# Power attention layer: the repeated, unread decay product is left out

## The chip, the core and the metric

One core of one Trainium2 chip. The metric is the time of one execution on the device in microseconds (us), the median of several; lower is better. The core has five engines that run side by side: TensorE (PE in the profile; PEld is its weight load), VectorE (DVE), ScalarE (ACT), GpSimd (POOL) and SyncE (SP, which here only issues DMAs). They wait for each other through semaphores.

## What is computed

Four layers one after the other on 16 batches of 256 tokens with 128 features: softmax attention with 16 heads, a gated mixture of 8 experts with its own attention, a "power" attention, and a capped mixture of 7 experts. The change touches the third alone:

```python
S = einsum('bhtd,bhsd->bhts', Q, K)                  # 16 heads of 8 features
Tm = 2 * log(abs(S) + EPS) + log(scale)              # power 2 of the score
Z = Tm + log_G[..., :, None] - log_G[..., None, :]   # decay: sums of log-sigmoid gates
Z = where(tril, Z, -inf)
P = exp(Z - rowmax(Z)); norm = sum(P)
O = einsum('bhts,bhsd->bhtd', P, V) / norm
x = x + layernorm(O)
```

## The kernel before, in words

The power layer (`power_layer`) goes through its batches in sixteen steps t = 0 to 15 (NB is 16), and each step through eight units u = 0 to 7 of two heads; n = 8 t + u numbers the units. A unit works on tiles of 128 x 512 elements of near blocks (keys in the same 128 tokens as the query) and 128 x 256 of far ones:

- TensorE forms the logarithms of the decays in one of two banks `decay_ps`: `decays(n)` (L1542, L1543) first writes a mask into the whole bank (a product of the identity in `cstb` with the causal mask `late`, both bf16), and `near_blocks(n)` (L1560) adds four small products of 32 rows, row differences of the cumulated gates, between them the near scores (L1564) in `score_ps`. `far_scores(n)` (L1578) adds the far ones.
- ACT takes the exponential of the bank into one of four buffers `E` (L1235).
- DVE takes the absolute value of the scores into `A` (L1419), 768 columns at once, and ACT squares it into `PT` (L1223). The squares stand for the exponential of 2 log|S|.
- POOL multiplies the near part of `PT` with `E` (L993).
- TensorE multiplies the weights with the values (`times_v`, L1597), two units at a time, and DVE copies the sums out (`OS`, L1317). They are turned (L1516) and normed.

TensorE's order in a unit is: `far_scores(n)`, `decays(n + 1)`, `near_blocks(n + 1)`, then what `POWER_AT` puts there for other batches (turning, projections, cumulated gates, router), `times_v`, and guests. `far_scores(n)` and `near_blocks(n + 1)` wait until DVE has taken the scores of unit n - 1; `decays(n + 1)` waits until ACT has read its bank two units ago. Each engine works in the order in which its code is written. The guests are the end of the layer before (gathers on POOL, sums on DVE, norms on ACT), spread over steps 0 to 10.

In `decays`, the product that writes the mask is made more than once in most steps: once more in steps 0 to 9, not in steps 10 to 13, twice more in steps 14 and 15. Each of these products starts a new accumulation (`start=True`) in the same bank, with the same operands, so that the next one overwrites it and nobody reads it.

Of the kernel before, what the change touches and what calls it, by code (L numbers as in the profile page):

```python
# [40 lines left out]
P = 128  # L41
NB, S, D = 16, 256, 128
# [791 lines left out]
def power_layer(nc, low, weighted_in, top, take, X, cst, cstb, QK, Vx, w, Y, chosen, router, bias, yd, wi, wo, gated, dram):  # L834
# [2 lines left out]

    NU, NE, NA, NW, WD, WU = H // 2, 4, 4, 12, 4 * P, 6 * P
    EXPERTS, EARLY, END = 7, (NB - 3) * TC, NB - 1
    STEPS, AGAIN, EARLY_CS = range(NB + 5), 2, 2  # L840
    UNITS = gated.UNITS
    with ExitStack() as ctx:
        def sb(name, shape, dt):
# [3 lines left out]
        def pb(name, banks):  # L847
            return ctx.enter_context(nc.psum_tensor(f"{name}P", [P, banks, 512], F32))
# [5 lines left out]
        decay_ps = pb("decay_ps", 2)  # L854
# [112 lines left out]
        def reach(eng, sem, count):  # L967
            if count > 0:
                eng.wait_ge(sem, count)
# [541 lines left out]
        def tensor(pe, guests):  # L1511
# [20 lines left out]
            late = cstb[:, P:2 * P].unsqueeze(1).to_broadcast([P, 4, P])  # L1532

            def decays(n):
                t, u = n // NU, n % NU
                if n < 2:
                    pe.wait_ge(gated.s_sg, UNITS - 1 + n)
                if u == 0:
                    pe.wait_ge(s_m, 96 * (t + 1))
                reach(pe, s_taken, n - 1)  # L1540
                for _ in range(AGAIN if t >= NB - 2 else t < 10):
                    pe.matmul(decay_ps[:, n % 2, :], cstb[:, 0:P], late, start=True, stop=True)  # L1542
                pe.matmul(decay_ps[:, n % 2, :], cstb[:, 0:P], late, start=True, stop=False)  # L1543

            def near_blocks(n):
# [36 lines left out]
            def times_v(t, g):  # L1582
# [16 lines left out]
                last.then_inc(s_pv, 1)  # L1599

            decays(0)
            near_blocks(0)
            guests[-1, 7]()
            for t in STEPS:
                for u in range(NU):
                    n = NU * t + u
                    if n < NU * NB:
                        far_scores(n)
                    if n + 1 < NU * NB:
                        decays(n + 1)  # L1610
                        near_blocks(n + 1)
# [1362 lines left out]
def build(nc, dram, out):  # L2974
    with ExitStack() as ctx:
# [21 lines left out]
        with ExitStack() as c1:  # L2997
# [34 lines left out]
            yd = nc.dram_tensor("tokens", [NT, D + 2], F32).ap()  # L3032
            od = nc.dram_tensor("expert_outputs", [2 * NT + P, D], F32).ap()
            power = power_layer(nc, Region(nc, front, back), weighted_in, Region(nc, small.at, region.end), take, X,
                                cst, cstb, QK, Vx, weights[2], XB, chosen, w["router1"], w["bias1"], yd, wi, wo, gated,
                                dram)
# [177 lines left out]
```

## Time and profile before

| | |
|---|---|
| time, median of 3 runs | 1105.17 us (1102.54 to 1108.28) |
| time of the profiled execution | 1104.22 us, span of its instructions 1102.3 us |
| mean granted clock of TensorE | 0.962 of full speed |
| power layer, first to last score | 670 to 951 us |
| PE busy over the span | 992.7 us (90%) |
| DVE busy | 850.8 us (77%) |
| ACT busy | 774.9 us (70%) |
| POOL busy | 637.9 us (58%) |

The profile is of one execution; its own time is the one to which sums of its rows are compared. Times in its rows are microseconds from the start of the span. Matmuls overlap in the systolic array and their ends are modelled: two that start 0.2 us apart may each last 0.4, so for TensorE the distance from start to start tells what one costs.

### The profile page before, as it was taken

The numbers are of one execution on the slowest core, as the hardware profiler recorded it, in microseconds if no ns is written. First come the engines' busy times: TensorE is split into PE (matmuls) and PEld (weight loads), VectorE is DVE, ScalarE is ACT, GpSimd is POOL, SyncE is SP. The second block draws the span as 40 slices with busy tenths as digits, with TensorE's granted clock in tenths as the row PEclk, the third lists the DMA queues.
The fourth block names the chain that finished last, engine by engine and source line by source line (L and its number), as shares of the span: only waits on it lengthen the run. The fifth ranks groups of instructions, "written<-read, shape, count | busy, mean of one in ns | idle before, by whom it ended". The sixth has DMA issues, their size and how long they took to land. (4 is left out here: it accounts for less than half of the span.)

```text
span 1102.3 us, 30949 instructions
## 1 busy us (share of the span) xinstructions
PE 992.7 (90%) x10503; PEld 586.9 (53%) x10503; DVE 850.8 (77%) x2252; ACT 774.9 (70%) x1760; POOL 637.9 (58%) x710
## 2 busy tenths in 40 slices
PE   4899999999999988988999998999999999848975
PEld 2344444444444443436998875555555565534752
DVE  3789999999999998954756767888989987772324
ACT  1578888888888877884554665788888998642405
POOL 4235544555443333760476838799888887526753
PEclk9999999999999999998999998999999999858988
DMA  5022222211111111220444421112121121141227
GB/s 133 26 58 77 77 73 77 77 55 40 41 41 40 41 33 43 59 70 20 132 124 132 134 75 41 48 43 66 44 61 32 36 58 52 40 164 41 53 74 198
DMA packets 114423, 75.24 MB, mean 68 GB/s; under 512 B 21335, under 2 KB 107808, under 8 KB 114272
## 3 DMA queue, kind: packets, MB, share of 16 engines
q1 hardware_dynamic: 105840, 54.68, 18.2%
q0 software_dynamic: 7744, 18.13, 5.5%
q8 instruction: 90, 1.47, 0.6%
q14 instruction: 61, 0.50, 0.2%
q10 hardware_dynamic: 688, 0.46, 0.1%
HBM read 26.75 MB, written 26.51 MB: 48 GB/s over the span
## 5 line engine op out<-in xcount | busy, mean ns | idle before, releaser
L637 DVE TENSOR_REDUCE mxsS<-scoreS 128x2 f32<-128x512 f32 x512 | 327.7, 685 | 40.9 <-PE scoreS L779 37.2
L519 ACT ACTIVATE PTS<-stS 128x512 f32<-128x512 f32 x512 | 284.1, 595 | 55.4 <-PE stS L783 54.2
L779 PE MATMUL scoreS<-QK 31*128 31x256 f16 x1024 | 171.6, 280 | 30.6 <-DVE mxsS L637 16.5
L993 POOL TENSOR_TENSOR PTP<-PTP,EP 128x512 f32<-128x512 f32 x128 | 163.3, 1280 | 38.7 <-ACT PTP L1223 37.7
L783 PE MATMUL stS<-QK 32*128 32x256 f16 x1024 | 169.4, 278 | 2.3 <-ACT PTS L519 2.3
L701 PE MATMUL pvS<-PTS,Vx 128*32 128x256 f32 x2048 | 142.0, 396 | 0.4 <-ACT PTS L519 0.2
L779 PEld LDWEIGHTS scoreS<-QK 31*128 31x128 f16 x1024 | 52.7, 93 | 152.6 <-DVE mxsS L637 105.5
L1419 DVE TENSOR_SCALAR AP<-score_psP 128x768 int32<-128x768 int32 x128 | 121.7, 951 | 12.1 <-PE score_psP L1578 10.6
L1223 ACT ACTIVATE PTP<-AP,epsP 128x768 f32<-128x768 f32 x128 | 118.9, 929 | 6.8 <-DVE AP L1419 6.5
L392 POOL TENSOR_TENSOR rsS<-veS,halfS 128x2 f32<-128x2 f32 (+1 forms) x32 | 33.0, 1031 | 154.0 <-DVE veS L605 87.1
L1235 ACT ACTIVATE EP<-decay_psP 128x512 f32<-128x512 f32 x128 | 75.7, 592 | 29.1 <-PE decay_psP L1560 27.4
L2175 POOL DMA_INDIRECT sorted<-gy,gidx x64 | 62.0, 969 | 41.5 <-DVE gowner L2537 22.8
L701 PEld LDWEIGHTS pvS<-PTS,Vx 128*32 128x32 f32 x2048 | 54.5, 111 | 51.0 <-issue 23.0
L2318 PE MATMUL gdown_ps<-down_w,gprod 128*128 (+1 forms) x496 | 65.7, 276 | 3.4 <-DVE XB L2573 3.1
L2318 PEld LDWEIGHTS gdown_ps<-down_w,gprod 128*128 128x128 f32 x496 | 60.1, 192 | 5.3 <-issue 4.4
L2645 DVE TENSOR_TENSOR gprod<-gsg,gup_ps 128x512 f32<-128x512 f32 x62 | 42.5, 686 | 22.2 <-ACT gsg L2430 10.9
L2187 POOL DMA_INDIRECT ggot<-mixed,gidx x48 | 46.7, 973 | 21.7 <-issue 13.3
L2367 ACT ACTIVATE ghTs<-gturn_ps,norm 128x256 f16<-128x256 f32 x46 | 21.8, 473 | 50.3 <-PE gturn_ps L2257 49.5
L783 PEld LDWEIGHTS stS<-QK 32*128 32x128 f16 x1024 | 51.9, 93 | 6.2 <-ACT PTS L519 3.1
L1560 PEld LDWEIGHTS decay_psP<-MP 32*128 32x128 bf16 x512 | 28.5, 93 | 48.6 <-issue 44.1
L398 POOL TENSOR_SCALAR yS<-X,mvS,rsS 128x128 f32<-128x128 f32 x64 | 50.6, 797 | 1.7
L1564 PE MATMUL score_psP<-QK 31*128 31x128 f16 x512 | 50.6, 218 | 0.0
(399 smaller groups left out, 2310.7 us busy)
## 6 DMA issues: line engine op xcount, KB each, us to landing
QK<-HLS SPq DMA_DIRECT2D x384, 32.0 KB
QK<-HLP SPq DMA_DIRECT2D x192, 32.0 KB
gsin<-sorted SPq DMA_DIRECT2D x46, 128.0 KB
mixed<-gob SPq DMA_DIRECT2D x46, 128.0 KB
sorted<-ggot POOLq DMA_DIRECT2D x22, 256.0 KB, 2.7
expert_outputs<-tzero SPq DMA_DIRECT2D x8, 512.0 KB
cgot<-expert_outputs SPq DMA_DIRECT2D x16, 256.0 KB, 5.4
tokens<-XB SPq DMA_DIRECT2D x16, 128.0 KB
```

Of the source, the lines that this page charges most:

```text
L398: last = pool.tensor_scalar(y[:, c, :], rows_of(X, b)[c], mv[:, c, 0:1], rs[:, kind, c:c + 1], ALU.subtract, ALU.mult)
L519: act.activation(PT[:, n % NPT, :], st_ps[:, (NS * t + n) % 3, :], ACT.Exp, scale=SCALE).then_inc(s_exp, 1)
L637: dve.tensor_reduce(mxs[:, u // 4, :, at], score_ps[:, n % 2, :].rearrange("p (c s) -> p c s", c=TC), AX.X, ALU.max).then_inc(s_max, 1)
L701: last = pe.matmul(pv_ps[32 * j:32 * j + 32, q], Vx[:, t % 3, c, 4 * g + j, :], PT[:, (4 * g + (j ^ 2)) % NPT, S * c:S * c + S], start=(c ...
L779: scored = pe.matmul(score_ps[:, k, cols], QK[part, new, g, 0, rows], QK[part, new, g, 1, :], start=True, stop=True)
L783: turned = pe.matmul(st_ps[:, (NS * t + n) % 3, cols], QK[part, old, g, 1, rows], QK[part, old, g, 0, :], start=True, stop=True)
L993: eng.tensor_tensor(w, w, E[:, n % NE, :], ALU.mult).then_inc(s_wd if n % NU in MULT_BY_DVE else s_wp, 1)
L1223: act.activation(PT[:, n % NW, :], A[:, n % NA, :], ACT.Square, bias=eps[:, 0:1]).then_inc(s_sq, 1)
L1235: act.activation(E[:, n % NE, :], decay_ps[:, n % 2, :], ACT.Exp).then_inc(s_taken, 1)
L1419: dve.tensor_scalar(A[:, n % NA, :].bitcast(I32), score_ps[:, n % 2 * WU:n % 2 * WU + WU].bitcast(I32), 0x7FFFFFFF, None, ALU.bitwise_and) ...
L2175: pool.indirect_dma_start(tables[h], bass.IndirectOffsetOnAxis(ap=idx[h][:, c, t:t + 1], axis=0), y[:, tiles[h].start + t, :], None).then_ ...
L2318: last = pe.matmul(down_ps[:, x % 2, t * D:(t + 1) * D], prod[:, x % NPROD, c * SLOTS + t * P:c * SLOTS + (t + 1) * P], down_flat[:, colum ...
```

## The change

The additional mask products are no longer issued, in whatever step; the one that starts the accumulation stays. The constant that told their number goes too.

```diff
-    STEPS, AGAIN, EARLY_CS = range(NB + 5), 2, 2
+    STEPS, EARLY_CS = range(NB + 5), 2
...
             def decays(n):
                 t, u = n // NU, n % NU
...
                 reach(pe, s_taken, n - 1)
-                for _ in range(AGAIN if t >= NB - 2 else t < 10):
-                    pe.matmul(decay_ps[:, n % 2, :], cstb[:, 0:P], late, start=True, stop=True)
                 pe.matmul(decay_ps[:, n % 2, :], cstb[:, 0:P], late, start=True, stop=False)
```

On TensorE, a unit in one of the first ten steps, before the change. `cstb` is the mask product's identity, `MP` the gates' rows:

```order
L1578 MATMUL score_psP<-QK 128x128 x2
L1542 MATMUL decay_psP<-cstb 128x512
L1543 MATMUL decay_psP<-cstb 128x512
L1560 MATMUL decay_psP<-MP 128x128
L1564 MATMUL score_psP<-QK 128x128
```

Such a row of L1542 stands there 80 times. On TensorE again, the first unit of step 14 in the program, before, with the values' product ahead of it:

```order
L1597 MATMUL pvP<-PTP,VkP 32x128 x4
L1578 MATMUL score_psP<-QK 128x128 x2
L1542 MATMUL decay_psP<-cstb 128x512 x2
L1543 MATMUL decay_psP<-cstb 128x512
L1560 MATMUL decay_psP<-MP 128x128
```

And the same place of the changed program, whose lines behind the edit have moved up by two (L1541 is the old L1543):

```order
L1595 MATMUL pvP<-PTP,VkP 32x128 x4
L1576 MATMUL score_psP<-QK 128x128 x2
L1541 MATMUL decay_psP<-cstb 128x512
L1558 MATMUL decay_psP<-MP 128x128
L1562 MATMUL score_psP<-QK 128x128
```

Only the rows of L1542 are gone, 80 single ones and 16 double ones, 112 products. Nothing else stands elsewhere on any engine.

## Rows read from the trace of the kernel before

**Rows 1.** The page, part 2: granted clock in 40 slices, tenths.

```profile
PEclk9999999999999999998999998999999999858988
```

**Rows 2.** Windows by step (1 to 6, 11, 13, 14, 15): length, then busy us (instructions) of PE, PEld, DVE, ACT, POOL; clock, DMA, GB/s.

```profile
692.41:709.70 17.29, 15.85 (x205) 8.75 (x197) 15.33 (x32) 14.39 (x31) 14.09 (x12) 1.00 0.11 29
709.70:726.53 16.83, 16.83 (x223) 9.45 (x223) 14.18 (x33) 14.00 (x30) 15.49 (x15) 1.00 0.20 52
726.53:743.81 17.28, 16.96 (x223) 9.44 (x223) 16.28 (x47) 15.27 (x35) 16.14 (x17) 1.00 0.20 50
743.81:762.13 18.32, 17.71 (x229) 10.09 (x229) 15.60 (x40) 16.62 (x39) 17.19 (x17) 1.00 0.21 56
762.13:780.98 18.85, 18.40 (x238) 10.32 (x237) 17.16 (x47) 15.96 (x35) 16.60 (x16) 1.00 0.21 53
780.98:798.37 17.39, 17.08 (x225) 9.87 (x220) 16.38 (x50) 15.08 (x35) 15.73 (x16) 1.00 0.21 56
...
870.11:886.28 16.17, 16.07 (x221) 9.95 (x220) 14.63 (x40) 14.76 (x35) 13.07 (x13) 1.00 0.14 36
...
902.52:918.92 16.40, 16.30 (x223) 10.08 (x223) 14.26 (x35) 15.54 (x34) 14.10 (x13) 1.00 0.20 53
918.92:936.36 17.44, 17.44 (x227) 9.46 (x227) 13.84 (x33) 13.45 (x27) 12.30 (x11) 1.00 0.22 61
936.36:950.71 14.35, 14.35 (x202) 7.73 (x202) 11.14 (x26) 11.67 (x21) 10.47 (x11) 1.00 0.10 24
```

**Rows 3.** Groups of TensorE's instructions by line and shape: count, busy us, mean ns.

```profile
L1543 PE MATMUL decay_psP<-cstb 128*128 128x512 bf16 x128 | 49.1, 384 | 0.0
...
L1542 PE MATMUL decay_psP<-cstb 128*128 128x512 bf16 x112 | 41.2, 392 | 0.0
```

**Rows 4.** TensorE in order of time, first unit of step 7: start, length in us.

```profile
798.05 0.28 PE L1578 MATMUL score_psP<-QK 31*128 31x128 f16 x2
798.26 0.39 PE L1542 MATMUL decay_psP<-cstb 128*128 128x512 bf16 x1
798.49 0.38 PE L1543 MATMUL decay_psP<-cstb 128*128 128x512 bf16 x1
...
800.29 0.28 PE L1578 MATMUL score_psP<-QK 31*128 31x128 f16 x2
```

**Rows 5.** The same of step 11, which has no repeated product.

```profile
869.79 0.28 PE L1578 MATMUL score_psP<-QK 31*128 31x128 f16 x2
870.01 0.39 PE L1543 MATMUL decay_psP<-cstb 128*128 128x512 bf16 x1
...
871.82 0.28 PE L1578 MATMUL score_psP<-QK 31*128 31x128 f16 x2
```

**Rows 6.** TensorE in order of time: far scores of step 0, and two of step 7.

```profile
682.63 0.28 PE L1578 MATMUL score_psP<-QK 31*128 31x128 f16 x2 [3.48 <-DVE AP L1419]
...
684.89 0.39 PE L1578 MATMUL score_psP<-QK 31*128 31x128 f16 x2 [0.91 <-DVE AP L1419]
...
689.42 0.39 PE L1578 MATMUL score_psP<-QK 31*128 31x128 f16 x2
...
811.70 0.28 PE L1578 MATMUL score_psP<-QK 31*128 31x128 f16 x2 [0.61 <-DVE AP L1419]
...
814.69 0.28 PE L1578 MATMUL score_psP<-QK 31*128 31x128 f16 x2
```

**Rows 7.** Windows around changes of the clock, columns as in rows 2.

```profile
382.99:386.40 3.41, 2.26 (x24) 1.14 (x26) 1.92 (x6) 1.82 (x5) 0.00 (x0) 1.00 0.18 50
386.40:389.81 3.41, 3.41 (x31) 1.68 (x30) 2.83 (x5) 2.44 (x5) 0.00 (x0) 0.50 0.03 9
...
683.36:690.19 6.83, 5.92 (x53) 3.17 (x52) 3.43 (x10) 3.96 (x9) 6.18 (x7) 0.50 0.10 25
...
864.27:867.68 3.41, 2.19 (x24) 1.51 (x27) 2.90 (x6) 2.98 (x5) 3.41 (x4) 1.00 0.06 14
```

**Rows 8.** Waits in the power layer: who waited for whom, us in total, times, longest.

```profile
PE score_psP L1578 <- DVE AP L1419: 9.9, 14, 3.5
```

## The prediction

> **What bounds the kernel now.** The first view is the page's second part, for TensorE's clock [rows 1]: it is whole in the slices of the power layer but for the one in which the layer starts, and low behind its end. The windows by step [rows 2] give each step's length and what each engine was busy in it; steps 7 to 9 repeat steps 4 to 6 to within 0.05 us. TensorE is busy nearly all of each step (17.71 of 18.32 us in step 4), but so are its modelled ends, and DVE, ACT and POOL stand at 15.60 to 17.19 in the same step. So shares alone don't tell who sets the pace. The order in time does: in step 7 the product of a far score starts at 798.05 and the next one at 800.29, a unit of 2.24 us [rows 4]; in step 11, in which no product is repeated, the same unit takes from 869.79 to 871.82, 2.03 us [rows 5]. The 0.21 us between them is the repeated product. TensorE thus sets the pace in this unit and would in the others as long as nobody else is late. Somebody else is, now and then: TensorE waited for DVE's absolute values 14 times in the layer, 9.9 us [rows 8], 3.48 us of it at once in step 0 [rows 6].
>
> **What the change removes.** 112 products of 128x512: ten steps of eight units with one, two steps with two, and the rows by line count the 112 [rows 3]. Nothing is moved and no wait is added; DVE, ACT, POOL and the DMA queues get the same instructions. The product left behind it clears the bank for the accumulation as before.
>
> *Price of one.* Not its 392 ns [rows 3], which overlap with the next one: start to start it is 798.26 to 798.49, 0.23 us [rows 4], and the two units above differ by 0.21. I take 0.21. If every one counted, 112 x 0.21 = 23.5 us; six of the eight in step 0 don't, since DVE is behind there (the waits of 3.48 and 0.91 us) [rows 6]. Upper bound of the gain: 106 x 0.21 = 22.3 us.
>
> (The Trainium skill, "TensorE: Matmul & The Clock Gate", section Back-to-back issue gap, gives 131 ns for each product of 512 columns in a sustained stream. By it the 112 would be 14.7 us instead of 23.5. This trace doesn't agree: its products of 512 columns start 230 ns apart.)
>
> *What takes over.* A step can't be shorter than its busiest in-order engine plus what that engine waits. The steps without the product show that rest: step 13 took 16.40 us with ACT busy 15.54, 0.86 above; step 11 took 16.17 with ACT busy 14.76, 1.41 above, and there TensorE still set the pace [rows 2]. So 0.86 is the better floor, and 1.41 the cautious one. I count DVE and ACT; POOL may fall up to four units behind (four decay buffers), and its mean over steps 1 to 6, 15.9 us, is below all floors but that of step 2. New length = the larger of (length - products x 0.21) and (busiest + 0.86):
> - step 1: 17.29, floor 15.33 + 0.86 = 16.19: gain 1.10
> - step 2: 16.83, floor 15.04, TensorE alone 16.83 - 1.68 = 15.15: gain 1.68
> - step 3: floor 16.28 + 0.86: gain 0.14
> - step 4: 18.32, ACT 16.62 + 0.86 = 17.48: 0.84; step 5: 18.85, DVE 17.16 + 0.86 = 18.02: 0.83; step 6: 17.39, DVE 16.38 + 0.86: 0.15. Steps 7 to 9 the same. Together 3.64
> - step 14 (two products a unit, 16 x 0.21 = 3.36 at most): 17.44, floor 13.84 + 0.86 = 14.70: 2.74
> - step 15: 14.35, ACT 11.67 + 0.86 = 12.53: 1.82
> - step 0: the two units in which TensorE was ahead: 0.4.
>
> Sum 11.5 us. With 1.41 for 0.86 the same sum is 0.55 + 1.24 + 0 + 2 x (0.29 + 0.28 + 0) + 2.19 + 1.27 + 0 = 6.4 us. Between 6.4 and 22.3 I take 11.5: the floors of four engines that lean on each other are seldom beaten.
>
> *Does it arrive at the end?* Behind the layer the last batch is routed and sorted before the experts can start; nothing there has a fixed time, so I pass the gain on whole. Where the low clock behind the layer ends may shift against the work, a us or two either way.
>
> *The clock.* The product also kept TensorE busy. In this trace the clock fell at 386.40 after 3.41 us of which TensorE was busy 2.26, and came back 3.41 us later [rows 7]; it fell at 683.36 after the 3.48 us wait and stayed at 0.50 (1.2 of 2.4 GHz) for 6.83 us [rows 6, 7]. In step 10, without a repeated product, TensorE was busy only 2.19 of 3.41 us (from 864.27) and the clock stayed [rows 7]. Both outcomes for about the same load: the steps that will look like step 10 (4 and 7, which have the same guests) are near the edge, while steps 11 and 13 ran without the product at 1.00 throughout. The price of a stretch of 3.41 us at half speed: a unit of step 0 took 4.53 us in the low clock (684.89 to 689.42) against 2.99 in step 7 (811.70 to 814.69), 0.34 us per us, 1.16 a stretch [rows 6]; at most half the stretch, 1.7. The unit of step 7 held four more transposes, so I take 1.5. I expect two such stretches more than now: 3.0 us back.
>
> Forecast: 11.5 - 3.0 = 8.5 us less than the 1104.2 of the profiled execution: 1095.7. That execution lies 1 us below the median shown; against this the same gain gives 1096.7, well inside the range.
>
> **The rivals.**
> - *TensorE alone was the bound.* All four engines slide together and nearly every product counts: 106 x 0.21, less a us or two of clock: 1082 to 1089, the middle 1084. For it: units repeat to 0.01 us between steps, as rows 4 and 5 show for one, though DVE is busy 91% of step 5. Against it: DVE 17.16 and ACT 16.62 leave no room for 1.68 us less in steps 5 and 4. Chance 0.10.
> - *Another wait takes the place.* The floor is 1.41, the gain 6.4, and two to four stretches of low clock take most of it: 1100.8, within 1099.7 to 1110.7. For it: steps 3, 6 and 9 are only 1.0 above DVE already. Chance 0.20.
> - *The clock falls again and again: slower.* The idle stretches are now a fifth of a us longer in every unit in which TensorE waits for DVE. If it fell once in each of the sixteen steps: 16 x 1.5 = 24, less 11.5: 1116.7. It decides from eight falls (8 x 1.5 = 12 > 11.5), and it is slower by over 0.5% from twelve. For it: the load before the fall at 386.40 was that of step 10. Against it: steps 11 and 13 never lost it, since TensorE, being the bound, closes up when a product goes. Chance 0.20.
> (The Trainium skill, the same page, section on the clock gate, says that the throttled state is the default and activity releases it, and so speaks against taking out filler work. By this rule the fall at 683.36 agrees, and the whole clock in step 11 shows that the filler isn't needed everywhere.)
> - *Forecast,* 1089 to 1099.7: chance 0.50.
>
> **How the numbers follow.** A measurement of this kernel tells 0.5% (5.5 us) from no change. Faster by more: 0.50 + 0.10 less the edges, 0.59. Within: 0.21. Slower by more: 0.20. The range reaches from 1085 (half of the first rival is left out) to 1111 (most of the third is): 0.05 + 0.15 outside. The forecast's own range is 1089 to 1099.7.
>
> **What the profile will show.** Right: the unit of rows 4 takes 2.03 us or a little more; steps 4 to 9 are 0.1 to 0.9 us shorter, steps 14 and 15 together 4.5; DVE's and ACT's idle times before their power lines shrink and TensorE's waits for DVE grow over 9.9 us; the windows show at most three more stretches at 0.50. Wrong: if steps 4 to 9 lose 1.7 us each, the floors were false; if clock below 1.00 stands in most steps, the price was the product's other use; if the steps shorten and the end doesn't, something behind the layer has a time of its own.

## The result and the profile after

| | before | changed |
|---|---|---|
| time, median of 19 runs each | 1104.0 us (1101.84 to 1111.08) | 1112.71 us (1102.34 to 1122.33) |
| ratio, 95% interval | | 1.0053 [1.0034, 1.0071] |
| profiled execution | 1104.22 us, span 1102.3 | 1122.33 us, span 1120.4 |
| its mean granted clock | 0.962 | 0.932 |

The kernel became slower by half a per cent, where 1095.7 us was forecast and 1111 was the upper end. The changed kernel spreads over 20 us from run to run, twice as much as before, and its time goes with the granted clock: 1102.34 us at 0.951, 1112.71 at 0.940, 1122.33 at 0.932. The profiled execution is the slowest of the 19, so more of it was lost to the low clock than usual; the changed kernel was therefore profiled again (below, the run called "Again"), with four of the five falls in the same places. The ratios leave out executions over 1.5% above the fastest of their kernel, here that slowest one and one of the kernel before beside the last four experiments (1213.88 us at a clock of 0.744). This ratio isn't the quotient of the two medians, which is 1.0079.

The page of the changed kernel, first part and the clock in 40 slices, beside [rows 1]:

```profile
span 1120.4 us, 30725 instructions
PE 1000.6 (89%) x10391; PEld 598.3 (53%) x10391; DVE 855.4 (76%) x2252; ACT 777.4 (69%) x1760; POOL 637.2 (57%) x710
...
PEclk9999999999999998979999998799696799958988
```

TensorE has fewer instructions and is busy for longer, 1000.6 us against 992.7. That can't be work; it is the same work at a lower clock. Slices 26, 29, 31 and 32, in the power layer, hold new digits below 9. The windows by step, of steps 0, 1, 3, 5, 6, 9, 10, 11, 14 and 15, with the columns of [rows 2]:

```profile
672.17:694.63 22.46, 15.01 (x163) 8.38 (x162) 19.51 (x41) 13.39 (x24) 19.62 (x18) 0.85 0.14 37
694.63:716.65 22.02, 21.02 (x182) 12.23 (x182) 14.53 (x33) 14.73 (x31) 12.96 (x11) 0.61 0.11 27
...
731.99:750.84 18.85, 16.92 (x215) 10.56 (x214) 16.32 (x48) 16.30 (x36) 18.36 (x18) 0.91 0.18 48
...
768.12:787.71 19.59, 17.90 (x255) 10.96 (x254) 18.83 (x47) 16.90 (x37) 18.54 (x17) 1.00 0.23 58
787.71:811.68 23.97, 22.97 (x186) 13.48 (x186) 16.74 (x49) 15.71 (x35) 15.66 (x15) 0.57 0.17 42
...
848.53:872.93 24.40, 23.40 (x186) 13.82 (x186) 16.76 (x50) 16.20 (x35) 13.63 (x13) 0.55 0.11 28
872.93:894.17 21.24, 20.02 (x221) 12.07 (x220) 15.91 (x40) 15.80 (x37) 14.27 (x13) 0.79 0.10 25
894.17:910.33 16.16, 16.05 (x221) 9.95 (x220) 14.62 (x40) 14.47 (x34) 12.00 (x12) 1.00 0.13 33
...
942.54:957.55 15.01, 14.08 (x211) 8.53 (x210) 13.69 (x34) 13.92 (x28) 11.54 (x12) 1.00 0.26 68
957.55:970.32 12.77, 11.52 (x187) 6.84 (x186) 11.05 (x26) 11.86 (x22) 10.69 (x10) 1.00 0.14 35
```

The sixteen steps take 298.15 us; before they took 279.94. The difference of 18.2 is that of the two executions (1122.33 - 1104.22 = 18.1), so as good as the whole of it arose in this layer (which starts 1.4 us later, and what is behind it is 1.5 shorter). Two kinds of steps are to be told apart. Steps 14 and 15 are 4.0 us shorter than before (27.78 against 31.79 [rows 2]), and step 11, which lost nothing, takes what it took. Steps 1, 6, 9 and 10 are 4 to 7 us longer, and their clock reads 0.55 to 0.79. Step 5 stands apart: its clock is whole, and yet it is 0.74 longer than in [rows 2], with DVE busy 18.83 us instead of 17.16 (step 8 is its copy, 19.58).

The stretches of low clock and those between them, by windows, beside [rows 7]:

```profile
697.60:714.70 17.10, 17.10 (x148) 10.09 (x147) 10.10 (x21) 11.07 (x24) 11.96 (x10) 0.50 0.07 19
714.70:745.40 30.70, 28.66 (x402) 16.98 (x396) 28.54 (x76) 26.06 (x54) 27.17 (x26) 1.00 0.19 50
745.40:748.80 3.40, 3.40 (x36) 2.81 (x36) 1.66 (x5) 3.15 (x9) 3.40 (x4) 0.50 0.10 24
...
789.80:810.30 20.50, 20.50 (x160) 12.10 (x158) 13.34 (x41) 13.75 (x32) 14.25 (x14) 0.50 0.16 39
...
851.20:878.50 27.30, 27.30 (x221) 15.67 (x220) 18.52 (x54) 18.04 (x40) 15.55 (x15) 0.50 0.11 29
...
888.70:892.10 3.40, 3.40 (x36) 2.80 (x36) 1.52 (x4) 3.17 (x9) 3.40 (x5) 0.51 0.15 37
```

Together 71.7 us at 0.50, where before there was none behind 690.19. In them TensorE is busy without a gap and in the three long ones DVE, ACT and POOL are busy 57 to 70% of the time: there TensorE, at 1.2 GHz, alone sets the pace. What stands ahead of the falls? TensorE in order of time, its far scores with the wait before them, and at the end the unit that answers to [rows 4]:

```profile
695.63 0.28 PE L1576 MATMUL score_psP<-QK 31*128 31x128 f16 x2 [1.89 <-DVE AP L1419]
...
788.71 0.28 PE L1576 MATMUL score_psP<-QK 31*128 31x128 f16 x2 [1.79 <-DVE AP L1419]
...
811.36 0.28 PE L1576 MATMUL score_psP<-QK 31*128 31x128 f16 x2
...
813.39 0.28 PE L1576 MATMUL score_psP<-QK 31*128 31x128 f16 x2
```

At full clock the unit takes 2.03 us, as forecast. Behind step 0 TensorE waits for DVE for more than 1.1 us seven times: in step and unit 1/1 (1.89), 3/5 (1.25), 4/6 (1.23), 6/1 (1.79), 7/6 (1.22), 9/1 (1.78) and 10/6 (1.22). Each of the five falls follows one of them within 2.5 us: 1/1, 3/5, 6/1, 9/1 and 10/6. Before, behind step 0, only one wait was that long (10/6). For the whole layer the row of [rows 8] (9.9 us) becomes 20.6; then the same row from 690 us to the layer's end, changed and before:

```profile
PE score_psP L1576 <- DVE AP L1419: 20.6, 22, 4.3
...
PE score_psP L1576 <- DVE AP L1419: 14.9, 18, 1.9
...
PE score_psP L1578 <- DVE AP L1419: 5.3, 11, 1.2
```

Why is DVE 1.8 us late at 6/1? DVE and then POOL in order of time at the end of step 5, changed kernel:

```profile
785.27 2.52 DVE L2584 SCALAR_TENSOR_TENSOR XB<-ggot_late,gW,XB 128x128 f32<-128x128 f32 x2
787.71 0.94 DVE L1419 TENSOR_SCALAR AP<-score_psP 128x768 int32<-128x768 int32 x1
...
785.07 2.57 POOL L993 TENSOR_TENSOR PTP<-PTP,EP 128x512 f32<-128x512 f32 x2
```

And the same place before:

```profile
780.13 0.92 DVE L2586 SCALAR_TENSOR_TENSOR XB<-ggot_late,gW,XB 128x128 f32<-128x128 f32 x2
780.98 0.94 DVE L1419 TENSOR_SCALAR AP<-score_psP 128x768 int32<-128x768 int32 x1
...
779.36 1.28 POOL L993 TENSOR_TENSOR PTP<-PTP,EP 128x512 f32<-128x512 f32 x1
781.04 1.28 POOL L993 TENSOR_TENSOR PTP<-PTP,EP 128x512 f32<-128x512 f32 x1 [0.40 <-ACT PTP L1223]
```

The two sums are guests, the end of the layer before (block 6 here, block 7 in step 8). Before, POOL had a gap between two products in which the second sum ran in 0.34 us. Now the product that ACT releases comes earlier, POOL works through without a gap, and the two sums take 2.52 us together, as long as POOL's two products in the same time. DVE takes the next scores 1.6 us later, and TensorE waits.

The long wait at 1/1 has the same cause. DVE, POOL in order of time at the start of step 1, changed kernel:

```profile
692.44 2.19 DVE L2584 SCALAR_TENSOR_TENSOR XB<-ggot,gW,XB 128x128 f32<-128x128 f32 x4
...
693.21 1.27 POOL L993 TENSOR_TENSOR PTP<-PTP,EP 128x512 f32<-128x512 f32 x1 [0.54 <-ACT PTP L1223]
```

And the same place before:

```profile
691.29 1.13 DVE L2586 SCALAR_TENSOR_TENSOR XB<-ggot,gW,XB 128x128 f32<-128x128 f32 x4
...
692.48 1.27 POOL L993 TENSOR_TENSOR PTP<-PTP,EP 128x512 f32<-128x512 f32 x1 [1.47 <-ACT PTP L1223]
```

Before, the four sums were over when POOL's product began; now they meet it and take 1.06 us longer, and TensorE's wait at 1/1 grows from 0.61 to 1.89.

### The profile page after: what moved, and what is told of

Same layout as the page of the kernel before. It is cut to its first block and busy times, and to the rows that moved or that the text cites. A ratio compares the mean times of both kernels' runs of the same rounds, so it can differ in the third digit from the quotient of the medians.

```text
span 1120.4 us, 30725 instructions
## 1 busy us (share of the span) xinstructions
PE 1000.6 (89%) x10391; PEld 598.3 (53%) x10391; DVE 855.4 (76%) x2252; ACT 777.4 (69%) x1760; POOL 637.2 (57%) x710
## 3 DMA queue, kind: packets, MB, share of 16 engines
q8 instruction: 89, 1.46, 0.5%
## 5 line engine op out<-in xcount | busy, mean ns | idle before, releaser
L1576 PE MATMUL score_psP<-QK 31*128 31x128 f16 x256 | 38.2, 232 | 21.3 <-DVE AP L1419 20.6
L1562 PE MATMUL score_psP<-QK 31*128 31x128 f16 x512 | 54.7, 231 | 0.0
L1558 PE MATMUL decay_psP<-MP 32*128 32x128 bf16 x512 | 54.6, 231 | 0.0
```

Source lines behind the costliest of these rows:

```text
L1562: pe.matmul(score_ps[:, o:o + P], QK[band, t % 3, g, 1, rows], QK[band, t % 3, g, 0, rows], start=True, stop=True)
```

## The experiments

The theories, after the result. *The clock:* the time is lost to long stretches at half speed, each set off by one wait of TensorE for DVE, and the sums that collide with POOL's products make the two most costly ones. *A fixed cost per step:* the repeated product served a timing in every step, so its return anywhere gives the time back. *Not the clock:* DVE and POOL collide more, and the low clock is only a sign of that. Each diff is against the changed kernel, except that a loop returned is shown alone. The first four were timed beside the kernel before on one chip, the next four on a second and the last four on a third, so each is to be judged by its ratio to the kernel before.

**Late part alone** (product kept in steps 0 to 9, gone in 14 and 15).

```diff
+                for _ in range(t < 10):
+                    pe.matmul(decay_ps[:, n % 2, :], cstb[:, 0:P], late, start=True, stop=True)
```

> The repeated product stays in steps 0 to 9 and goes in steps 14 and 15 only. Theory A (the time was lost because TensorE's clock fell in steps 0 to 10, and only there): 4.5 us faster than before, about 1099.5, no stretch of low clock in the power layer beyond the one at its start, steps 14 and 15 at about 15.0 and 12.6 us. Theory B (a product less costs the clock wherever it is left out): stretches of low clock in steps 14 and 15, no gain or slower, 1104 to 1108.

Measured: 1099.4 us against 1104.44, ratio 0.9949 [0.9923, 0.9975]. Steps 14 and 15 by windows:

```profile
924.18:939.19 15.01, 14.08 (x211) 8.53 (x210) 13.69 (x33) 13.93 (x28) 11.56 (x12) 1.00 0.25 67
939.19:951.99 12.80, 11.53 (x187) 6.84 (x186) 11.06 (x27) 11.88 (x22) 10.73 (x10) 1.00 0.14 33
```

They are those of the changed kernel to 0.03 us. This part of the change is a gain of 4.0 us in the two steps and 5.0 by the medians (5.6 by the ratio), and arrives at the end. In one point theory A missed: the clock also fell at 871.8, for 3.4 us, behind the wait of 1.23 us at 10/6, where the program is that of before.

**Early part alone** (gone in steps 0 to 9, kept twice in 14 and 15).

```diff
+                for _ in range(AGAIN if t >= NB - 2 else 0):
+                    pe.matmul(decay_ps[:, n % 2, :], cstb[:, 0:P], late, start=True, stop=True)
```

> The repeated product goes in steps 0 to 9 and stays, twice, in steps 14 and 15. Theory A: slower than before by the loss of the whole change plus the 4.5 us that steps 14 and 15 gave, so 1110 to 1120, with low clock in several of steps 0 to 10. Theory B: the loss is shared, 1106 to 1108.

Measured: 1117.07 us, ratio 1.0080 [1.0047, 1.0114]. The early part carries the whole loss. Its profile shows the pair of sums at 1226 and 1357 ns, and 54.6 us at half clock in the layer behind 690, in five stretches, one of them behind each collision: 789.2 to 799.4 and 847.2 to 867.7.

**One more** (two additional products in steps 0 to 9 and in 14, 15: 80 more than before).

```diff
+                for _ in range(AGAIN if t >= NB - 2 or t < 10 else 0):
+                    pe.matmul(decay_ps[:, n % 2, :], cstb[:, 0:P], late, start=True, stop=True)
```

> One more product than before in steps 0 to 9 (two repeated ones), else as before: the price of one product while the clock is whole. Theory A (each costs TensorE, which sets the pace, 0.21 us): 80 x 0.21 = 17 us slower, about 1121, and the clock no worse than before. Theory C (the product is half hidden behind other engines' work): 5 to 9 us slower. If the product gives back clock even here, less than 5.

Measured: 1120.62 us, ratio 1.0124 [1.0091, 1.0157]. 16.2 us for 80 products is 0.20 each (by the ratio 13.7 us, 0.17 each), and a unit of step 4 takes 2.46 us (two products more than the 2.03 of [rows 5]):

```profile
750.05 0.28 PE L1578 MATMUL score_psP<-QK 31*128 31x128 f16 x2
750.26 0.61 PE L1542 MATMUL decay_psP<-cstb 128*128 128x512 bf16 x2
...
752.51 0.28 PE L1578 MATMUL score_psP<-QK 31*128 31x128 f16 x2
```

The price of a product holds. The sums collide here as well (935 and 1357 ns), yet the clock shows no fall in the layer behind 692. TensorE's waits behind step 0 are shorter there than in the changed kernel, 1.27 us at the most; whether that or the products themselves kept the clock, this run doesn't tell.

**Without the colliding sums.** The second half of the second sum of blocks 6 and 7 is left out of the computation (unit 7 of steps 5 and 8), and the first half gives the signal that the sum is ready.

```diff
-            if some.stop == TB:
+            if some.stop == (2 if c == 1 and b in range(EARLY, 8) else TB):
...
-                    after.update({(t, 3): tail(("add0a", b)), (t, 4): tail(("add0b", b)), (t, 6): tail(("add1a", b)),
-                                  (t, 7): tail(("add1b", b))})
+                    after.update({(t, 3): tail(("add0a", b)), (t, 4): tail(("add0b", b)), (t, 6): tail(("add1a", b))})
```

> The changed kernel, and the second half of the second sums of the last two blocks of the layer before (two operations of DVE in unit 7 of steps 5 and 8, each) is left out of the computation. In the changed kernel they took 2.5 us against 0.92 before, while POOL worked through two power products, and TensorE then waited 1.8 us before its clock fell in step 6 and in step 9. Theory D (that pile-up sets off the two long falls): no low clock from step 6 unit 1 to step 10 unit 0, a stretch of 40 to 48 us less at half speed, 1095 to 1104. Theory E (a lower load as such makes the clock fall, here or a little later): the falls stay, a few us at most below the changed kernel, 1108 to 1114.

Measured: 1095.69 us, ratio 0.9900 [0.9869, 0.9930]. Four sums gone, 2 us of DVE's work at the pace of before, make 17 us of difference to the changed kernel. Windows from the first fall on:

```profile
692.80:706.50 13.70, 13.03 (x102) 7.05 (x106) 8.91 (x20) 9.65 (x21) 8.22 (x7) 0.50 0.07 19
706.50:863.40 156.90, 146.48 (x2008) 89.78 (x2001) 146.57 (x385) 142.28 (x314) 142.00 (x132) 1.00 0.20 50
863.40:866.80 3.40, 3.40 (x35) 2.42 (x34) 1.06 (x3) 2.97 (x8) 3.40 (x5) 0.51 0.16 40
```

The long falls of steps 6 and 9 are gone. This takes work away, though; the next run only moves it.

**The sums moved** one unit ahead, nothing left out.

```diff
-                    after.update({(t, 3): tail(("add0a", b)), (t, 4): tail(("add0b", b)), (t, 6): tail(("add1a", b)),
-                                  (t, 7): tail(("add1b", b))})
+                    after.update({(t, 3): tail(("add0a", b)), (t, 4): tail(("add0b", b)), (t, 6): tail(("add1a", b), ("add1b", b))})
```

> The changed kernel with all its work; the second half of those sums stands one unit earlier on DVE (unit 6 of steps 5 and 8), where in the changed kernel's trace POOL runs operations of one input. Theory D (the pile-up of those sums with POOL's products sets off the long falls): the sums take 0.3 to 0.5 us each, steps 6 and 9 keep the clock, 1096 to 1103. Theory E (leaving the work out had lowered DVE's load, and that alone helped): at least one of the two falls stays, 1108 to 1114.

Measured: 1098.38 us against 1103.98, ratio 0.9944 [0.9920, 0.9969]. A sum takes 371 or 340 ns in unit 6, and steps 6 and 9 keep the clock. Falls remain at 694.2 (13.7 us), 813.7 (3.4) and 940.0 (10.2). The one of 3.4 gives a price: unit 7/6 takes 4.09 us with it, and 4/6, the same unit of a step with the same guests, 2.78 without, 1.3 us. The one at 940.0 has no long wait ahead of it: TensorE had waited 0.27 us at 939.66.

**The sums moved, and the product back in steps 0 and 1.**

```diff
+                for _ in range(t < 2):
+                    pe.matmul(decay_ps[:, n % 2, :], cstb[:, 0:P], late, start=True, stop=True)
```

> As the kernel before: sums one unit earlier, and the repeated product in steps 0 and 1 only. If the product in step 1 is what keeps the clock from 697 us on, the low stretch of 13.7 to 17.1 us that followed there in the runs without it is gone: 2 to 5 us faster than with the sums moved alone, about 1094. If the fall there comes anyway, no difference to the sums moved alone.

Measured: 1097.67 us, ratio 0.9940 [0.9925, 0.9955], no different from the run before. The fall at the start came anyway, at 698.4 (10.2 us); two more are at 742.8 (6.8) and 852.0 (3.4). A miss: the product in these units doesn't protect step 1. What stands ahead of the fall is again a collision, of another guest: an operation of DVE on four columns, which took 0.16 us before and runs beside POOL's product here. DVE, then POOL:

```profile
694.17 1.25 DVE L2607 SCALAR_TENSOR_TENSOR gnm<-gmv,grs 128x4 f32<-128x4 f32 x1
...
694.11 1.29 POOL L993 TENSOR_TENSOR PTP<-PTP,EP 128x512 f32<-128x512 f32 x1 [1.27 <-ACT PTP L1223]
```

TensorE then waited 1.71 us at 1/1.

**Half a product** (256 columns in steps 0 to 9).

```diff
+                for _ in range(t < 10):
+                    pe.matmul(decay_ps[:, n % 2, 0:2 * P], cstb[:, 0:P], late[:, 0:2, :], start=True, stop=True)
```

> Steps 0 to 9 repeat half of the product (256 columns), steps 14 and 15 nothing. If the price goes by columns and the clock holds: 80 x 0.105 = 8.4 us less than with the whole product there (1099.4 measured), limited by DVE's and ACT's floors to 3 to 6: 1093 to 1096. If half doesn't keep the clock or the sums pile up as in the changed kernel: 1105 to 1114.

Measured: 1103.85 us, ratio 0.9993 [0.9963, 1.0022]. The sums still collide (1225 and 1367 ns), and the falls behind them are at 783.5 (6.8 us) and 841.5 (10.2); a third, at 872.2 (3.4), follows the wait at 10/6. Half the product, shorter stretches, no gain in the end.

**The product in two steps alone** (5 and 8, those of the collisions; the sums not moved).

```diff
+                for _ in range(t in (5, 8)):
+                    pe.matmul(decay_ps[:, n % 2, :], cstb[:, 0:P], late, start=True, stop=True)
```

> The repeated product in steps 5 and 8 alone, the sums where they were. Theory D with timing (the product keeps TensorE slow enough there that POOL isn't behind when the sums come): the pair of sums takes 0.9 to 1.2 us, the falls in steps 6 and 9 are gone, 1098 to 1105. Theory E (it takes a load in all steps): falls elsewhere, 1108 to 1114.

Measured: 1101.03 us, ratio 0.9965 [0.9938, 0.9992]. The pair is fast again, 660 and 340 ns:

```profile
783.69 0.92 DVE L2586 SCALAR_TENSOR_TENSOR XB<-ggot_late,gW,XB 128x128 f32<-128x128 f32 x2
```

Behind the first 13.7 us, two stretches of 3.4 us remain, at 797.5 and 852.1, in steps 6 and 9 after all, behind waits of 0.80 us and 0.3 us. The two long ones are gone. The product's use in these steps was the rhythm: with it, POOL's gap meets the second sum. The median is 11.7 us below that of the changed kernel; by the two ratios it is 0.0088 x 1104 = 9.7 us.

**Products only where TensorE waits** (the changed kernel with 41 unread products ahead of the far scores of the seven units that wait over 1.1 us; the sums collide as before).

```diff
+            FILL = {(1, 1): 7, (3, 5): 5, (4, 6): 5, (6, 1): 7, (7, 6): 5, (9, 1): 7, (10, 6): 5}
...
+                    if FILL.get((t, u)):
+                        reach(pe, s_taken, n)
+                        for _ in range(FILL[t, u]):
+                            pe.matmul(decay_ps[:, (n + 1) % 2, :], cstb[:, 0:P], late, start=True, stop=True)
```

> The changed kernel, with 41 unread products put only where its TensorE waited over 1.1 us for DVE: seven ahead of the far scores of units 1/1, 6/1 and 9/1, five at 3/5, 4/6, 7/6 and 10/6 (step/unit), less than the wait each. Nothing else is touched, so the waits themselves and the pile-up of the sums stay. Theory F (it is TensorE's idleness in those seven waits that makes the clock fall): no low clock between 690 and 955 us but for an odd stretch of 3.4, 1093 to 1099. Theory G (the mean load per step decides): long falls as in the changed kernel, 1108 to 1115.

Measured: 1097.67 us against 1104.82, ratio 0.9933 [0.9912, 0.9954]. TensorE and DVE in order of time at 6/1, and step 6 by windows:

```profile
777.97 1.68 PE L1609 MATMUL decay_psP<-cstb 128*128 128x512 bf16 x7
...
779.81 0.28 PE L1576 MATMUL score_psP<-QK 31*128 31x128 f16 x2 [0.15 <-DVE AP L1419]
...
776.37 2.51 DVE L2589 SCALAR_TENSOR_TENSOR XB<-ggot_late,gW,XB 128x128 f32<-128x128 f32 x2
...
778.80:796.03 17.23, 15.48 (x190) 9.13 (x188) 16.23 (x49) 14.36 (x33) 14.34 (x14) 1.00 0.21 54
```

DVE is as late as in the changed kernel (2.51 against 2.52 us), and the far scores don't start sooner for it; but the wait is filled, 0.15 us of it are left, the clock stays whole and the step takes 17.23 us instead of 23.97. Only two stretches of 3.4 us remain in the layer, at 826.6 and 833.4, behind waits of 0.4 to 0.8 us that weren't filled. This tells the clock from the collision: step 5, with the collision and a whole clock, takes 19.56 us, 1.9 more than without the collision (17.70 in the next run), and in step 6 the low clock had cost 23.97 - 17.23 = 6.7.

**The sums moved and the waits filled** (35 products by the list below and by the trace; the expectation miscounts them as 37). The loop of the run before and the edit of "the sums moved" stand beside this list.

```diff
+            FILL = {(1, 1): 7, (3, 5): 5, (4, 6): 4, (6, 0): 2, (6, 5): 3, (7, 6): 4, (9, 0): 2, (9, 5): 3, (10, 6): 5}
```

> The same idea on the kernel with the sums one unit earlier, 37 products in its own waits. By theory F the best version: no long fall, the sums 0.3 to 0.5 us each, 1090 to 1095. By theory G as with the sums moved alone, 1098.

Measured: 1093.75 us, ratio 0.9893 [0.9872, 0.9915], faster than both kernels. The layer from 692.80 to 942.00 by windows, then steps 1, 5 and 6 of it:

```profile
692.80:942.00 249.20, 240.98 (x3283) 145.89 (x3278) 229.98 (x589) 226.67 (x490) 218.59 (x202) 1.00 0.19 50
...
695.83:711.30 15.47, 14.62 (x186) 8.58 (x183) 14.13 (x31) 14.38 (x31) 12.92 (x12) 1.00 0.11 28
761.53:779.23 17.70, 16.72 (x223) 10.12 (x222) 16.94 (x48) 16.04 (x36) 16.73 (x16) 1.00 0.26 60
779.23:796.70 17.47, 16.93 (x224) 10.16 (x223) 16.42 (x50) 15.38 (x36) 16.11 (x16) 1.00 0.23 57
```

There is no low clock in it at all. The sixteen steps take 269.24 us, 10.7 less than before.

**Again** (the changed kernel once more).

> The changed kernel once more, on the chip of the others, as it is. Its pair of sums in steps 5 and 8 takes 2.5 us again if the order of the engines sets it and not chance; the low clock behind units 1/1, 6/1 and 9/1 is then seen again, 1105 to 1115.

Measured: 1110.3 us (1107.36 to 1115.92), ratio 1.0051 [1.0029, 1.0072]. In its profiled execution (1115.05 us) four of the five falls stand in the same places, with other lengths; behind the wait of 1.28 us at 3/5 none came. The windows of three:

```profile
786.00:806.50 20.50, 20.50 (x160) 12.10 (x158) 13.39 (x41) 13.75 (x32) 14.31 (x14) 0.50 0.15 39
847.50:857.70 10.20, 10.20 (x79) 6.07 (x83) 7.91 (x24) 6.54 (x17) 5.92 (x6) 0.50 0.07 21
878.20:885.00 6.80, 6.80 (x58) 4.51 (x56) 3.52 (x8) 4.37 (x11) 5.40 (x6) 0.50 0.15 39
```

With the 13.7 us at 693.9 it has 51.2 us at half clock against 71.7, and is 7.3 us faster. What differs between these two executions is above all how long the clock stays low.

**Half a product, and the sums moved.** The edits of the two runs of these names together.

> Half of the product (256 columns) in steps 0 to 9, nothing in 14 and 15, and the sums one unit earlier. In the run with half the product the sums had taken 2.6 us again and the clock fell in steps 6 and 9, 1103.9. Theory D: without the pile-up it doesn't, and the half price shows: 1094 to 1097. If the half product itself is too little for the clock: 1100 or more.

Measured: 1093.95 us, ratio 0.9895 [0.9874, 0.9915], as good as the filled waits. Low clock only at 681.7 (6.8 us) and 695.4 (10.2).

**The theories, answered.** *Not the clock* is refuted by the products put only where TensorE waits: there the collisions stay, and the time comes back with the clock. *A fixed cost per step* is refuted by two runs: sixteen products in steps 5 and 8 gave back 9.7 us, and sixteen in steps 0 and 1 nothing. For *the clock*, here are all waits of TensorE for DVE ahead of a far score, behind step 0, in the fourteen profiled executions of thirteen kernels. Sixteen waits took 1.46 to 1.93 us, and the clock fell at every one of them or within 3 us behind it, once for 6.8 us and else for 10.2 to 27.3. Thirty-five took 1.14 to 1.29 us; behind ten of them it fell, for 3.4 or 6.8 us (3 of 7 at 3/5, none of 7 at 4/6, 2 of 7 at 7/6, 5 of 12 at 10/6, neither of 2 elsewhere). Six more falls had only waits of 0.3 to 0.8 us ahead of them; five lasted 3.4 us, the one at 940.0 with the sums moved 10.2.

The fall at the start of the layer goes by the collision of step 1. In ten of the profiles either the four sums or the operation on four columns met POOL's product there and took 1.1 us longer. Eight of them then show a wait of 1.71 to 1.93 us at 1/1 and a fall; the two others had filled that wait, and no fall. In the four others (before, late part alone, one more, half a product) nothing met it, the wait at 1/1 was 0.4 to 0.7 us, and no fall came.

## Why the prediction was wrong

- *The price of a product, 0.21 us:* right. The unit of [rows 4] became one of 2.03, and one product more in each unit cost 0.20 by the medians (0.17 by the ratio).
- *The sum of 11.5 us:* right in size for a kernel that keeps its clock. With the sums moved and the waits filled, the layer is 10.7 us shorter. Step by step against [rows 2]: step 1 1.82 (forecast 1.10), 2 1.49 (1.68), 4 1.09 (0.84), 5 1.15 (0.83), steps 14 and 15 4.0 (4.56); step 3 is 0.38 longer (0.14 shorter was forecast), step 0 0.94 longer (0.4 shorter), steps 6 and 9 0.1 longer (0.15 shorter), and step 13, which had no product to lose, 0.43 shorter. So the sum is near in part because misses offset each other. That kernel also holds 35 filling products and moved sums, so this bears the sum out as a whole and no single term exactly.
- *What the sum had overlooked:* that DVE's own work grows. The floor of step 5 was 17.16 + 0.86, with DVE's busy time taken as fixed. It became 18.83, since the sums collide with POOL's products in a new phase. Steps 5 and 8 came out at 19.59 and 19.58, where 17.70 and 17.69 stand without the collision: 2 x 1.9 = 3.8 us.
- *The step that failed: "I expect two such stretches more than now: 3.0 us back."* The profiled execution had 71.7 us at half clock, 21 times the length of the stretch that I priced. Step by step against the kernel with moved sums and filled waits, whose clock is whole, it lost 6.55 us in step 1, 1.19 in step 3, 6.50 in step 6, 6.94 in step 9 and 3.99 in step 10: 25.2 us, not 3.0. The price per us was near (25.2 / 71.7 = 0.35; from the units of step 0 I had 0.34, and a stretch of 3.4 us cost 1.3 where 1.5 was taken). The number of falls was nearer, five and not two (four in the second profile, 51.2 us in all). Their length was wrong: each stretch was taken to end after 3.41 us, as at 386.40 [rows 7], though the one at 683.36 had lasted twice that.
- The whole account: 11.5 forecast, 10.7 reached; less 3.8 for the collisions and 25.2 for the clock is -18.3, the 18.2 us by which the layer of the profiled execution is longer. The other executions of the changed kernel are shorter, and their clocks higher. The losses are read off as differences to the kernel with moved sums and filled waits, so the account has to add up; what the runs show is the split.
- *"Steps 4 and 7 are near the edge":* wrong place for this kernel. They waited for 1.2 us each and kept the clock in both of its profiles; the falls came behind the waits in steps 1, 3, 6, 9 and 10. Step 7 did lose it for 3.4 us in two other kernels (early part alone, sums moved), step 4 in none.
- *The third rival,* the clock falls again and again, had the mechanism and the sign. It had the wrong condition ("it decides from eight falls"): four or five sufficed, as a fall can last for more than a whole step. The rivals that DVE, or a wait, holds the rest of the gain back (1100.8) and that TensorE alone is the bound (1084) are both refuted by the kernel with moved sums and filled waits, at 1093.75: its layer is 10.7 us shorter, where they say 6.4 and 22.3.
- *"The product also kept TensorE busy"* was right, but it named half of the use. The product in steps 5 and 8 alone stopped the collisions by the rhythm that it set, and took 9.7 us off the changed kernel with 16 products.
- Most falls follow waits, and 41 products filled into the waits left two short ones; but once low, the clock stayed at 0.50 through all of the 27.3 us from 851.20 with TensorE busy without a gap. The Trainium skill, "TensorE: Matmul & The Clock Gate", section "A second HAM failure mode: psum-queue depth-cycling", tells of short idle stretches between groups of matmuls that make the clock swing between its two states, and section "What's actually happening" that activity releases the throttle. The traces agree with the first, and for the long stretches not with the second as it stands.

Not settled: what ends a stretch of low clock (3.4 us in some, 27.3 in one, in the same kernel), why a wait of the same 1.2 us costs the clock in one execution and not in another, and what sets whether DVE's guests meet POOL's product in step 1. It is a near thing: before, the operation on four columns began 0.14 us ahead of the product (692.34 against 692.48), with the sums moved and the product back in steps 0 and 1 it began 0.06 behind it (694.17 against 694.11), though the two programs are the same up to there. Each kernel but the changed one was profiled once, so this may be chance.

## What to carry to other kernels

An unread instruction on the engine that sets the pace has a price that a profile shows well, and two uses that it doesn't show: it holds the clock, and it holds the phase in which other engines meet. Before it goes, look for the places at which the pacing engine waits for a microsecond or more, and price a fall of the clock there by its possible length and not by the shortest one in the trace: here 10.2 to 27.3 us at half clock, but for one, behind waits of 1.5 us and more, and three times in ten 3.4 or 6.8 behind waits of 1.2. Look also at what the other engines run side by side, since an operation that now meets another can make such a wait. Then put back filler into the waiting units alone, and move the work that collides: here that turned a loss of 0.5% into a gain of 1.1%.

## What was unexpected of the hardware

- A DVE sum of 128x128 with two inputs in SBUF took 340 ns alone and 1236 and 1365 ns beside POOL's products of 128x512, as long as these themselves (1.28 us). Moved to the unit before, they took 340 to 371 ns. Even the operation on four columns went from 0.16 to 1.25 us. The Trainium skill, "SBUF — State Buffer", section "Who interferes with whom", says that a DVE instruction with two SBUF inputs contends with a GpSimd instruction that reads SBUF, and section "SBUF: two separate sides" that the other one then blocks for the whole instruction. The traces agree.
- Single waits of 1.8 us of an engine that was otherwise busy 9 us in 10 were followed by 20.5 and 27.3 us at half clock, with TensorE recorded busy throughout.
